# A graph network kernel on one core: each engine's program without its loop

## The reference

```python
# layer 0
h = relu(layernorm(x)); A = adj + I; d = A.sum(-1) ** -0.5
x = x + (A * d[:, None] * d[None, :]) @ (h @ W + b)
# layer 1: a hypergraph convolution, twice, with the same H
h = relu(layernorm(x)); H = adj != 0; w = adj[0, :]
Dn, Be = 1 / (H @ w), 1 / H.sum(0)
conv = lambda v: Dn[:, None] * (H @ (Be[:, None] * (H.T @ v)))
h = layer_norm(relu(conv(h @ W1.T) + b1)) * gamma + beta      # 512 -> 1024
x = x + conv(h @ W2.T) + b2                                   # 1024 -> 512
```

## Time and profile before

| | us |
|---|---|
| median of 3 runs | 2123.66 (2123.6 to 2125.76) |
| the profiled execution, its own time | 2124.24 |
| its span, first to last instruction | 2122.4 |
| busy: PE / DVE / POOL / ACT | 2074.2 / 1837.0 / 1448.1 / 1172.2 |
| mean granted TensorE clock | 0.995 |

### The profile page before, as it was taken

The page is one execution under the profiler, slowest core; times in us unless marked ns, Lnnn a source line. Parts: engine busy times, 40 slices in busy tenths (PEclk is TensorE's granted clock), DMA queues, the critical chain, the costliest instruction groups (busy, mean ns, idle before and its releaser), DMA issues.

```text
span 2122.4 us, 53623 instructions
## 1 busy us (share of the span) xinstructions
PE 2074.2 (98%) x15126; PEld 1154.5 (54%) x15126; DVE 1837.0 (87%) x4514; ACT 1172.2 (55%) x1969; POOL 1448.1 (68%) x2318
## 2 busy tenths in 40 slices
PE   4899999999999999999999999999999999999998
PEld 2455555555555555555555555555555555555554
DVE  5888888888888888888888888888888888888875
ACT  6555555555555555555555555555555555555553
POOL 3667767767766776777676776677677677677663
PEclk9999999999999999999999999999999999999999
DMA  4011111110011111111111111111111111111100
GB/s 148 30 34 33 43 35 33 38 40 33 33 43 35 33 43 35 33 42 36 33 38 40 33 33 43 35 33 43 35 33 43 35 33 38 40 33 33 43 27 21
DMA packets 58345, 82.13 MB, mean 39 GB/s; under 512 B 6736, under 2 KB 23120, under 8 KB 58320
## 3 DMA queue, kind: packets, MB, share of 16 engines
q1 hardware_dynamic: 58320, 81.82, 11.8%
HBM read 48.24 MB, written 33.55 MB: 39 GB/s over the span
## 4 chain that ended last, share of the span: by engine, by line
PE 92%; issue 2%; DVE 2%; DMA 1%; POOL 1%; SPq 1%; ACT 0%; DVEq 0%; POOLq 0%
PE ps_c L311 45%; PE ps_y L311 30%; PE ps_c L300 3%; PE ps_c L301 3%; PE ps_c L302 3%; PE ps_t L300 3%; PE ps_t L302 3%; PE ps_t L301 3%; DMA x_t<-in_x_dram 1%; PE ps_a L430 1%; PE ps_p L402 0%; DMA adj_t<-in_adj_dram 0%; DVE raw L605 0%; SPq L249 0%; PE ps_p L403 0%
## 5 line engine op out<-in xcount | busy, mean ns | idle before, releaser
L909 POOL TENSOR_TENSOR rd<-u,neg_half 128x2 f32<-128x2 f32 x128 | 138.0, 1078 | 225.5 <-DVE u L669 225.3
L504 ACT ACTIVATE P_hi<-ps_p 128x128 f16<-128x128 f32 x128 | 35.6, 278 | 447.9 <-PE ps_t L302 439.4
L466 ACT ACTIVATE h<-z 128x512 f32<-128x512 f32 x256 | 161.2, 630 | 201.3 <-DVE z L600 201.2
L481 ACT ACTIVATE hn_hi<-h,nm,sc 128x1024 f16<-128x1024 f32 x128 | 158.8, 1240 | 193.5 <-POOL nm L939 193.5
L311 PE MATMUL ps_c<-w1h,t1h 128*128 128x512 f16 x1024 | 263.3, 379 | 0.0
L311 PE MATMUL ps_c<-w1l,t1h 128*128 128x512 f16 x1024 | 263.3, 380 | 0.0
L311 PE MATMUL ps_c<-w1h,t1l 128*128 128x512 f16 x1024 | 262.8, 379 | 0.0
L600 DVE SCALAR_TENSOR_TENSOR z<-ps_c,dn,b_all 128x512 f32<-128x512 f32 x256 | 188.2, 735 | 73.8 <-PE ps_c L311 73.6
L311 PE MATMUL ps_y<-w2h,t2h 128*128 128x512 f16 x1024 | 243.5, 381 | 2.4 <-issue 2.4
L892 POOL TENSOR_TENSOR x1b<-x,b_all 128x512 f32<-128x512 f32 x128 | 162.3, 1268 | 120.0 <-DVE x L621 120.0
L311 PE MATMUL ps_y<-w2l,t2h 128*128 128x512 f16 x1024 | 242.0, 379 | 0.0
(11 more groups left out here) (139 smaller groups left out, 5829.0 us busy)
## 6 DMA issues: line engine op xcount, KB each, us to landing
x_t<-in_x_dram SPq DMA_DIRECT2D x128, 256.0 KB, 2.7
out_dram<-out_t SPq DMA_DIRECT2D x128, 256.0 KB, 2.1
adj_t<-in_adj_dram SPq DMA_DIRECT2D x128, 64.0 KB, 1.7
raw_w<-in_W1T_dram SPq DMA_DIRECT2D x4, 512.0 KB, 6.9
raw_w<-in_W2T_dram SPq DMA_DIRECT2D x8, 256.0 KB, 8.2
raw_w<-in_W_dram SPq DMA_DIRECT2D x4, 256.0 KB, 3.8
b_all<-in_b_dram SPq DMA_DIRECT2D x2, 256.0 KB, 6.6
b_all<-in_b_dram SPq DMA_DIRECT2D x1, 512.0 KB, 9.8
```

The source lines that it names most:

```text
L466: act.activation(h[:, cols], z[:, cols], ACT.Relu).then_inc(s_h[n], 1)
L481: act.activation(hn_hi[:, :], h[:, :], ACT.Identity, bias=nm2[:, m:m + 1], scale=sc2[:, m:m + 1])\
L909: pool.tensor_tensor(rd0[:, m, :], u0[:, m, :], neg_half[:, :], ALU.pow).then_inc(s_pp0, 1)
```

## The change

Every engine's `step` is called 134 times, and no loop is left. `i` is the number 0 everywhere, so waits compare with constants, and addresses are constants. Nothing else changes: each engine issues the same operations in the same order.

```diff
-    LOOP_FROM = 6
-    LOOP_TO = NG - 4
-    assert (LOOP_TO - LOOP_FROM) % 2 == 0 and LOOP_TO > LOOP_FROM
-    ORDER = list(range(-3, LOOP_FROM)), list(range(LOOP_TO, NG + 3))
+    ORDER = range(-3, NG + 3)
...
         def every_step(eng_type, step):
-            for k in ORDER[0]:
-                step(0, k)
-            with nc.Fori(0, LOOP_TO - LOOP_FROM, 2, engines=(eng_type,), hint_back_edge=True) as i:
-                step(i, LOOP_FROM)
-                step(i, LOOP_FROM + 1)
-            for k in ORDER[1]:
+            for k in ORDER:
                 step(0, k)
...
-            for k in ORDER[0]:
-                step(0, k)
-            with nc.Fori(0, LOOP_TO - LOOP_FROM - 4, 2, engines=(ENG.SP,), hint_back_edge=True) as i:
-                step(i, LOOP_FROM)
-                step(i, LOOP_FROM + 1)
-            for k in [*range(LOOP_TO - 4, LOOP_TO), *ORDER[1]]:
+            for k in ORDER:
                 step(0, k)
```

## The result

The changed kernel takes 2127.52 us (median of 14 runs, 2124.24 to 2132.3) against 2123.63 of the kernel before (14 runs on the same chip). The ratio is 1.0018 with an interval of [1.0011, 1.0025]: slower, by 3.9 us, where 8.9 were forecast. The profiled execution of it took 2132.3 us, the slowest of its 14, so its trace shows more loss than the median has.

What follows compares the result with a forecast made beforehand. PE's own matmuls were taken to bound the kernel, 16.03 us a step. 2124.24 - 5.9 (loop costs removed) + 14.9 (33 fetch meetings) = 2133.2 profiled, 2132.6 as median; whole range 2117.5 to 2147.

Steps and rivals of the forecast that it cites:

- The gains: Loop's end, steps and first step: 3.8 us, 1.4 us and 0.7 us won, together 5.9 us.
- The stop: DVE, second step behind the loop: 2.12 us idle ahead of line 656, a cost of leaving the loop; all goes.
- 1.6 of slow matmuls: Step behind the loop: `ps_y` at half rate after PE's 2.04 us wait, part of the 3.8 us to be won.
- The mechanism: Load of `x` near a step's end: PE's program fetches on q8 delay it by 1.0 us, so PE waits for `u`.
- The price of a meeting: A step whose fetch falls beside the load of `x`: PE loses 0.45 us each time.
- How often: Former loop's 118 steps: fetch moves two instructions a step, harmful from 11 to 15 us; 33 meetings, 14.9 us.
- PE's reserve: Time `u` is early for a step's first matmul: 0.17 us in the loop, about 0.5 in written-out code.
- The slow steps at its start: Start and end of the former loop: 30 or so neighbouring steps waiting for `u`, about 0.45 us each.
- the fetches are hidden: Rival, whole former loop: added fetches cost nothing, only the 5.9 us gain remains, 2117.8 us; chance 0.17.
- The rival of fewer meetings: Rival, former loop: 4 to 22 meetings costing 1.8 to 9.9 us, 2119.6 to 2127.7 us, no change; chance 0.23.
- The fetch that stays beside the transfer: Rival, all 118 steps: every one meets its fetch, costing 53 us, 2171 us; chance 0.08.
- Written-out code did not stop DVE: Rival judged here: DVE stops at about every second step, PE losing 3.8 us some 57 times, 2335 us; chance 0.04.

Runs made afterwards that it cites:

- e8: Kernel before, loops kept, with the load of `x` issued ahead of the store of `out_t`: 2115.99 us, ratio 0.9962.
- e1: The changed kernel itself, run once more for a second profiled execution: 2127.05 us, ratio 1.0020.
- e3: Kernel before with only PE written out, the other four engines keeping their loops: 2144.85 us, ratio 1.0099.
- e6: Changed kernel, steps padded to 256 PE instructions from step 6, 44 more once in step 6, holding the fetch beside the load of `x`: 2179.79 us, ratio 1.0263.
- e5: Changed kernel with two PE instructions added in each of steps 10 to 123, making 256, so the fetch stays at a harmless place: 2118.64 us, ratio 0.9971.
- e7: Changed kernel with SP issuing the load of `x` ahead of the store of `out_t`: 2114.78 us, ratio 0.9958.
- e2: Kernel before with only PE keeping its loop, the other four engines written out: 2118.99 us, ratio 0.9978.
- e4: Kernel before with only DVE written out, the others keeping their loops: 2121.39 us, ratio 0.9993.
- e10: Changed kernel with the padding that holds the fetch at the harmful place, plus the load of `x` ahead of the store: 2119.03 us, ratio 0.9977.

## Why the prediction was half right

**The gains: right.** 5.9 us were forecast; the loop's steps lose 2.7 us less and step 125 loses 3.8 less, 6.5 in all. The stop was DVE's, as said (only DVE written out: gone; only PE written out: still there). Its 3.8 us hold the delay of `x` too, though (e8), and the "1.6 of slow matmuls" of the sum are the clock at half for 3.4 us, which followed PE's longer idle time and did not come where that was 1.24 us.

**The mechanism: right.** PE's fetches on q8 delay the load of `x`, DVE is late with `u`, and PE waits. q8 was forecast with 127 packets and 2.1 MB and has 127 and 2.08, q14 with about 130 and has 135; the landing of `x` with 3.7 us inside and 2.6 outside the run of slow steps, which it is. Putting the fetch there in every step costs about 56 us (61 with the padding), putting it elsewhere nothing but one meeting of 1.8 us, and moving the load away from the end of the step takes it back.

**The price of a meeting: right, with a spread.** 0.45 us were taken; it was 0.44 in the typical execution (7.9 us over 18), 0.46 with the fetch held in place, and 0.58 in the first profile.

**How often: this step failed.** "I take the stretch from 11 to 15 us ... I take 33." There are 20 in the former loop (104 to 123), 18 of them met in the second execution. I took every place between the store and the landing of `x` for harmful, 84 instructions or 42 places of the lap of 127, and took nine off for the places not reached. In the changed kernel the fetches that cost PE something start from the issue of `x` to 1.3 us behind it. The outer parts of my stretch were free: at 1.8 us and more ahead of the issue the packet costs nothing (step 103, and steps 106 and 108 of e1), and in step 6 it starts at 137.2, 2.1 us behind the issue at 135.12, and costs nothing. In step 5 it starts 2.8 us behind and the load lands 0.65 late, within PE's reserve. What a fetch between 1.8 and 0.1 us ahead, or 1.3 and 1.9 behind, would do, no step of the changed kernel shows. The run goes from step 104 to the last load in step 125. Steps 3 and 4 are the same places as steps 130 and 131, and they are slow as the end of the same run, so the whole run is at most 28 of 127 places, not 42, and 20 of them fall into the former loop. The slow steps at its start, which I had expected, do not exist.

This boundary is not a law for other arrangements: with SP in its loop (e3) fetches 1.5 to 2.9 us behind the issue cost most of all.

With 20 for 33 the sum is 20 times 0.45, 9.0 us, less 6.5, or 2.5 us slower; the runs have 3.9 and 3.3. The profiled execution came out at 2132.3 where the sum said 2133.2, by chance: its meetings were dearer, and its start and end are 2.7 us longer.

**The rivals.** That the fetches are hidden holds for 98 of 118 steps and was false for the rest. The Trainium skill, page "Runtime: NRT & Kernel Launch", section "Instruction fetch mechanics", calls crossing a block "mostly hidden"; for PE itself the trace agrees, it shows no gap at a block's end anywhere in the former loop, but not for the loads beside it. The block of 16 KiB, which the prediction took from the same section, fits q8 alone (2.08 MB in 127 packets); the packets of q14 have half of that (1.11 MB in 135). The rival of fewer meetings, 4 to 22 with 2119.6 to 2127.7 us, is what happened, with another cause than I named: the fetch does move by two instructions a step, the harmful part is only shorter. The fetch that stays beside the transfer, forecast with 2171, did not occur in the changed kernel and is what e6 builds, with 2179.8. Written-out code did not stop DVE (`issue: 1.2` us in all ahead of its first operation, three places).

**What stays open.** In step 54 of the kernel before a load came late, and cost 0.5 us, with no fetch beside it. The 1.6 us of e5, in step 82, are a meeting at a rare price: the load is issued at 1354.48 and takes 4.7 us, a fetch starts 2.6 us behind the issue, at 1357.10, and the last packet of the load ends together with it, at 1358.18. The DMA queues of e5 from 1357.0 to 1357.2 us:

```profile
q8 instruction: 1, 0.02, 33.6%
```

Other fetches of e5 at 2.6 to 2.8 us behind the issue let the load land after 3.1 to 3.2 us; what makes the difference, here and in e3, is not known. Between steps 103 and 104 the start of the fetch moves by 1.9 us against the step, though only by two instructions, and in e1 it moves back and forth; I saw it and have no cause for it. And why a meeting is dearer in one execution than in another was not tried.

## What to carry to other kernels

Transfers of kind "instruction" are traffic: look where in a step they start, and what is issued at that moment. Here the long written-out program was harmless where the load had reserve (e7), and cost up to 56 us where it was needed as soon as it could land (e6). So give the load its reserve first: moving one load ahead of one store brought 12.3 us to the changed kernel and 8 to the kernel before, and the question of the loop then weighs 1.2 us. Since `u` does not read `x`, moving it ahead of DVE's wait for `x` might do the same; no run tried that.

When the number of instructions in a step is near that of a block, the fetch creeps through the step; count how many steps of a lap it spends at the harmful place, and bound that place by the steps that are seen to lose time (here steps 3 and 4 of the kernel before, and the one behind its loop), not by the whole life of the transfer.

## What the runs showed of the hardware

SP itself is held up in a meeting. Its issue of the load of `x`, all 128 in the changed kernel, then in the one with the early load (shortest, median, longest in ns):

```profile
L236 SPq DMA_DIRECT2D x_t<-in_x_dram x128: 328/367/1887, 1.2 to 2054.4; - x128
```

```profile
L236 SPq DMA_DIRECT2D x_t<-in_x_dram x128: 327/328/432, 1.2 to 2035.6; - x128
```

In 10 of the meetings from step 104 to 124 the issue takes 1.4 to 1.9 us instead of 0.37 (1.85 in step 114 above). These ten steps lose 0.84 us each, the other eleven 0.34. In the other execution it is nine, with 0.64, and twelve other steps, with 0.25: a held issue goes with a dearer meeting, but does not tell the two executions apart.

DVE, after it has left its loop, stops for 2.1 to 2.2 us in the second step behind it, in every kernel in which DVE has a loop and that was read there (before, e3, e8), and in none in which it has not (after, e2, e4). TensorE's clock is at half (0.50 to 0.53 in the rows, 1.2 GHz) for 3.4 us behind some of PE's idle times and not behind others: behind 2.04 us in the kernel before, 1.90 and 2.15 in e3, 3.2 in e6 and 3.3 in e10 (but not behind 1.91 in step 4 of e6), and behind 2.42 us at the end of two executions (after, e4) but not of the others with the same 2.42. Behind 1.24 us in e8 it stayed at full. Where `ps_y` fell into it, its eight matmuls of 512 columns took 3.2 to 3.5 us instead of 1.89; in step 14 of e3 the loss was 1.7 us.
